# Attention scores from two float32r parts on alternating halves of the array, in place of three bfloat16 parts on 72 rows

## What is computed

```python
h = _layernorm(x, axis=-1) * (1 + ca) + sa
q, k, v = (qkv[0], qkv[1], qkv[2])          # from h @ qkv_w + qkv_b, 16 heads of 8
q = _apply_rotary(q, rope)
k = _apply_rotary(k, rope)
scores = jnp.einsum('bhqd,bhkd->bhqk', q, k) * HD ** (-0.5)
scores = jnp.where(causal_mask, -jnp.inf, scores)
attn = jax.nn.softmax(scores, axis=-1)
out = jnp.einsum('bhqk,bhkd->bhqd', attn, v)
x = x + ga * (out @ out_w + out_b)          # then a second layer norm and the experts
```

## Time and profile before

| | us |
|---|---|
| median of 3 runs | 417.44 |
| lowest, highest | 413.38, 420.29 |
| the profiled execution: its time | 416.36 |
| the profiled execution: its span | 414.6 |
| PE, DVE, ACT, POOL busy in the span | 368.3, 269.7, 219.1, 101.4 |
| mean granted clock of PE, share of full speed | 0.934 |

### The profile page before, as it was taken

How to read it: one execution, slowest core, us unless ns; L and a number is a source line. 1 busy time by engine, 2 the same in 40 slices (tenths; PEclk the granted TensorE clock), 3 DMA queues, 4 the chain that set the end, 5 groups by cost and what they waited for, 6 DMA issues and landing times.

```text
span 414.6 us, 6917 instructions
## 1 busy us (share of the span) xinstructions
PE 368.3 (89%) x2383; PEld 169.0 (41%) x2383; DVE 269.7 (65%) x586; ACT 219.1 (53%) x415; POOL 101.4 (24%) x185
## 2 busy tenths in 40 slices
PE   6948864989879899899999988999999999999876
PEld 3424431444444244333243343444424444434544
DVE  3446781688677747777877777867787777333165
ACT  5240342456215624566767664745776666685333
POOL 3302554245410004232040301200203232213110
PEclk9988996799758959999999999989999999999989
DMA  7276172000110000233304040000000000000000
GB/s 259 97 195 122 64 206 64 3 2 2 63 40 2 0 0 4 90 93 85 91 4 113 3 114 2 3 2 25 3 0 3 4 2 3 3 1 2 25 2 26
DMA packets 12338, 18.87 MB, mean 46 GB/s; under 512 B 3600, under 2 KB 8592, under 8 KB 12176
## 3 DMA queue, kind: packets, MB, share of 16 engines
q1 hardware_dynamic: 12016, 18.04, 15.8%
q10 hardware_dynamic: 288, 0.39, 0.3%
HBM read 12.98 MB, written 5.24 MB: 44 GB/s over the span
## 4 chain that ended last, share of the span: by engine, by line
PE 71%; DVE 7%; issue 5%; ACT 5%; DMA 4%; SPq 4%; POOL 3%; POOLq 0%; ACTq 0%; DVEq 0%
PE ps_o L971 16%; PE ps_b L951 14%; PE ps_a L933 14%; PE ps_a L928 4%; PE ps_a L910 4%; PE ps_s L903 3%; PE ps_s L839 3%; PE ps_s L890 3%; SPq L389 3%; ACT pt L602 2%; DVE tmax L788 2%; DMA qst<-negt 2%; DVE rot L693 2%; PE ps_s L857 1%; PE ps_s L871 1%
## 5 line engine op out<-in xcount | busy, mean ns | idle before, releaser
L788 DVE TENSOR_REDUCE tmax<-ps_a 128x1 f32<-128x512 f32 (+3 forms) x304 | 187.5, 657 | 87.4 <-PE ps_a L933 86.9
L602 ACT ACTIVATE pt<-ps_b 128x512 f32<-128x512 f32 (+1 forms) x304 | 165.5, 573 | 125.2 <-PE ps_b L951 123.3
L951 PE MATMUL ps_b<-qst,kst 75*128 75x512 bf16 (+3 forms) x384 | 116.0, 336 | 12.8 <-DMA qst<-negt 7.7
L933 PE MATMUL ps_a<-kst,qst 72*128 72x128 bf16 (+3 forms) x576 | 118.4, 286 | 1.9 <-DVE tmax L788 1.7
L971 PE MATMUL ps_o<-pt,v_sb 128*32 128x512 f32 (+3 forms) x768 | 84.6, 514 | 0.4 <-POOL pt L498 0.3
L933 PEld LDWEIGHTS ps_a<-kst,qst 72*128 72x128 bf16 x576 | 51.5, 102 | 69.8 <-DVE tmax L788 37.2
L498 POOL TENSOR_SCALAR_AFFINE_SELECT pt<-pt 128x512 f32<-128x512 f32 x64 | 40.2, 636 | 86.6 <-ACT pt L602 86.4
L951 PEld LDWEIGHTS ps_b<-qst,kst 75*128 75x128 bf16 x384 | 35.0, 99 | 44.8 <-ACT pt L602 23.5
L910 PE MATMUL ps_a<-maska,identb 128*128 128x512 bf16 x96 | 29.4, 399 | 3.3 <-POOL maska L435 3.3
L928 PE MATMUL ps_a<-maska,identb 128*128 128x512 bf16 x64 | 26.5, 413 | 4.5 <-DMA kst<-kparts 2.6
L469 POOL CAST negp<-negm 128x16 bf16<-128x16 f32 x16 | 3.1, 196 | 110.7 <-DVE negm L714 110.6
(11 more groups left out here) (108 smaller groups left out, 311.4 us busy)
## 6 DMA issues: line engine op xcount, KB each, us to landing
qst<-qparts SPq DMA_DIRECT2D x48, 96.0 KB
kst<-kparts SPq DMA_DIRECT2D x48, 96.0 KB
qparts<-part SPq DMA_DIRECT2D x4, 384.0 KB, 2.6
kparts<-part SPq DMA_DIRECT2D x4, 384.0 KB, 2.8
xs<-in_x SPq DMA_DIRECT2D x4, 256.0 KB, 6.8
rope_sb<-in_rope SPq DMA_DIRECT2D x1, 1024.0 KB, 6.8
qparts<-part SPq DMA_DIRECT2D x4, 256.0 KB, 2.9
qst<-negt SPq DMA_DIRECT2D x48, 4.0 KB, 1.7
```

The source lines that it names most:

```text
L602: act.activation(pt[:, G % NP, h0:h0 + nh, 0:w], src, ACT.Exp, scale=SCALE).then_inc(s_exp, 1)
L788: dve.tensor_reduce(dst, src, AX.X, ALU.max).then_inc(s_max, 1)
L933: last = pe.matmul(dst[:, j * nk:(j + 1) * nk], qst[0:ROWS, half, h, r * P:r * P + P], kst[0:ROWS, kh, h, k0:k0 + nk], start=(kind != "dia ...
L951: last = pe.matmul(ps_b[:, n % 2, j * w:(j + 1) * w], kst[:, kh, h, kt * P:kt * P + P], qst[:, half, h, c0:HALF], start=True, stop=True)
```

## The change

`PARTS` goes from 3 to 2, and the parts are float32r, a four-byte type of the matmul, to which ACT and POOL round. Two parts of q against two of k give 32 rows a head; a row of zeros follows, and in pass B two rows of the maxima against rows of ones (33 and 35 rows). `qst` and `kst` are float32 now and span 128 partitions: even heads of a group lie from partition 0, odd heads from partition 64 (`a` is the half). A job of pass A and a bank of pass B hold heads of one half only, and the lists alternate: pass A takes half 0, 1, 0, 1, pass B 1, 0, 1, 0 (`ones`), so that in a slot the two stand on different halves. "diag" jobs cover two tiles of two heads instead of one tile of four. Two places that held four heads of 128 columns in one bank take two banks now (tri r=1, and the last key tile of pass B): 12 and 28 jobs a step, 320 of each pass in all.

Stages `q3` and `k3` are gone: two parts need one rounding on ACT and one subtraction. The later prep stages stand earlier in `plan` by as many slots. `load` issues 8 DMAs of 64 KB a group in place of 6 of 96 KB, `max_rows` 4 in place of 3. The rows of ones, which ACT wrote in 3.6 us each for the two halves, come by four DMAs from a small tile on ACT's queue. The transposition of the maxima (`max2`) is float32. Matmuls with v, the masks and all side stages keep their types.

```diff
 NG = H // HG
-PARTS = 3
-ROWS = PARTS * PARTS * HD
-ROWSM = ROWS + PARTS
+PARTS = 2
+SPLIT = PARTS * HD
+ROWS = PARTS * SPLIT
+ROWSA = ROWS + 1
+ROWSB = ROWSA + PARTS
+TILE = 64
+HP = H // 2
 VW = HD + 1
 VPAD = H * VW + 24
 SCALE = float(HD) ** -0.5
 EPS = 1e-5
-ONES = 1 + 0x3F80 / 2 ** 23
...
 def bank_jobs_a(half):
 
-    jobs = []
-    for r in range(TU):
-        jobs.append(("diag", r, 0, HG, P))
-        if r:
-            nh = min(HG, HALF // (r * P)) if r < 3 else 1
-            jobs += [("tri", r, h, nh, r * P) for h in range(0, HG, nh)]
-        if half:
-            jobs += [("sq", r, h, 1, HALF) for h in range(HG)]
+    jobs = [("diag", a, r, 0, 2, P) for r in range(0, TU, 2) for a in range(2)]
+    for r in range(1, TU):
+        nm = 2 if r < 3 else 1
+        jobs += [("tri", a, r, m, nm, r * P) for m in range(0, 2, nm) for a in range(2)]
+    if half:
+        jobs += [("sq", a, r, m, 1, HALF) for r in range(TU) for m in range(2) for a in range(2)]
     return jobs
 
 
 def groups_b(half):
 
     out = []
+    ones = [(2, 1), (0, 1), (3, 1), (1, 1)]
     if half:
-        out += [(kt, 0, 0, [(h, 1) for h in range(HG)]) for kt in range(TU)]
+        out += [(kt, 0, 0, ones) for kt in range(TU)]
     for kt in range(TU):
-        n = HALF - kt * P
-        nh = max(1, HALF // n) if n < 384 else 1
-        out.append((kt, half, kt * P, [(h, nh) for h in range(0, HG, nh)]))
+        out.append((kt, half, kt * P, ones if HALF - kt * P >= 384 else [(2, 2), (0, 2)]))
     return out
...
-PREP = {"norm1": 0, "nz": 2, "hT": 3, "q1": 3, "q2": 3, "q3": 3, "k1": 3, "k2": 3, "k3": 3, "v": 5}
+PREP = {"norm1": 0, "nz": 2, "hT": 3, "q1": 3, "q2": 3, "k1": 3, "k2": 3, "v": 5}
...
+        qst = sb("qst", [P, 2, HP, HALF])
+        kst = sb("kst", [P, 2, HP, HALF])
...
             if name in ("q2", "k2"):
                 i, n = (0, 1)[name == "k2"], prep_no[u]
                 eng.wait_ge(s_full[i], n + 1)
-                eng.wait_ge(s_part[i], 3 * n + 1)
-                eng.tensor_tensor(rot[i][:, 0], full[i][:, :], part[i][:, 0], ALU.subtract).then_inc(s_rem[i], 1)
-            if name in ("q3", "k3"):
-                i, n = (0, 1)[name == "k3"], prep_no[u]
-                eng.wait_ge(s_rem[i], n + 1)
-                eng.wait_ge(s_part[i], 3 * n + 2)
-                eng.tensor_tensor(part[i][:, 2], rot[i][:, 0], part[i][:, 1], ALU.subtract).then_inc(s_part[i], 1)
+                eng.wait_ge(s_part[i], 2 * n + 1)
+                eng.tensor_tensor(part[i][:, 1].bitcast(F32R), full[i][:, :], part[i][:, 0],
+                                  ALU.subtract).then_inc(s_part[i], 1)
...
-                    planes = (5, PARTS)[i]
-                    for p in range(PARTS):
-                        rows = bass.AP(tensor=src, offset=(w * planes * HD + p * step) * row + h0 * HALF,
-                                       ap=[[row, R], [1, HG * HALF]])
-                        sp.dma_start(dst[R * p:R * p + R, half, h0:h0 + HG, :].rearrange("p h t -> p (h t)"),
-                                     rows).then_inc(s_stack[half][g], 16)
+                    planes = (PARTS + 1, PARTS)[i]
+                    for a in range(2):
+                        for p in range(PARTS):
+                            rows = bass.AP(tensor=src, offset=(w * planes * HD + p * step) * row + (HP * a + 2 * g) * HALF,
+                                           ap=[[row, SPLIT], [1, 2 * HALF]])
+                            r = TILE * a + SPLIT * p
+                            sp.dma_start(dst[r:r + SPLIT, half, 2 * g:2 * g + 2, :].rearrange("p h t -> p (h t)"),
+                                         rows).then_inc(s_stack[half][g], 16)
...
-                M = HG * TU
-                for p in range(PARTS):
-                    dst = qst[ROWS + p:ROWS + p + 1, half, HG * g:HG * g + HG, :].rearrange("o h (r x) -> o (h r) x", x=P)
-                    sp.dma_start(dst, negt[M * p:M * p + M, s % 2, :]).then_inc(s_mstack[s % 2], 16)
+                for a in range(2):
+                    for c in range(PARTS):
+                        r, n = TILE * a + ROWSA + c, HP * (PARTS * a + c)
+                        dst = qst[r:r + 1, half, 2 * g:2 * g + 2, :].rearrange("o m (r x) -> o (m r) x", x=P)
+                        sp.dma_start(dst, negt[n:n + HP, s % 2, :]).then_inc(s_mstack[s % 2], 16)
...
             act.wait_ge(s_one, 1)
-            rows_of_ones(0)
+            for a in range(2):
+                r = TILE * a + ROWS
+                act.dma_start(kst[r:r + 1 + PARTS].rearrange("p f h t -> p (f h) t"),
+                              consts[:, :].unsqueeze(1).to_broadcast([1 + PARTS, 2 * HP, HALF])).then_inc(s_ones, 16)
+                act.dma_start(qst[r:r + 1].rearrange("p f h t -> p (f h) t"),
+                              consts[0:1, :].unsqueeze(1).to_broadcast([1, 2 * HP, HALF])).then_inc(s_ones, 16)
...
+                rows = slice(TILE * a, TILE * a + ROWSA)
+                tiles_of = [(q, m) for q in (r, r + 1) for m in range(2)] if kind == "diag" else \
+                    [(r, m0 + j) for j in range(nm)]
+                for j, (q, m) in enumerate(tiles_of):
+                    k0, kh = (q * P, half) if kind == "diag" else (0, half) if kind == "tri" else (0, 0)
+                    last = pe.matmul(dst[:, j * nk:(j + 1) * nk],
+                                     qst[rows, half, 2 * g + m, q * P:q * P + P].bitcast(F32R),
+                                     kst[rows, kh, 2 * g + m, k0:k0 + nk].bitcast(F32R), start=(kind != "diag"),
+                                     stop=True, skip_group_check=True)
...
+                if gi == 0 and (h0, nh) == groups_b(half)[0][3][0]:
+                    pe.wait_ge(s_mstack[s % 2], 64 * (s // 2 + 1))
                 if n >= 2:
                     pe.wait_ge(s_exp, n - 1)
                 for j in range(nh):
-                    h = HG * g + h0 + j
-                    last = pe.matmul(ps_b[:, n % 2, j * w:(j + 1) * w], kst[:, kh, h, kt * P:kt * P + P],
-                                     qst[:, half, h, c0:HALF], start=True, stop=True)
+                    a, m = divmod(h0 + j, 2)
+                    rows = slice(TILE * a, TILE * a + ROWSB)
+                    last = pe.matmul(ps_b[:, n % 2, j * w:(j + 1) * w],
+                                     kst[rows, kh, 2 * g + m, kt * P:kt * P + P].bitcast(F32R),
+                                     qst[rows, half, 2 * g + m, c0:HALF].bitcast(F32R), start=True, stop=True)
...
-                    c = (HG * g + j) * VW
+                    c = (HG * g + 2 * (j % 2) + j // 2) * VW
```

More of the change, by code:

```diff
@@ L26 @@
 F32 = mybir.dt.float32
+F32R = mybir.dt.float32r
 BF16 = mybir.dt.bfloat16
@@ L216, in adaln_block @@
         rank = sb("rank", [P, TU, NE])
-        ones = sb("ones", [P, 1])
+        consts = sb("consts", [1 + PARTS, HALF])
         mhalf = sb("mhalf", [P, TU])
@@ L239, in adaln_block @@
         full = [sb(f"full{i}", [P, HALF]) for i in range(2)]
-        part = [sb(f"part{i}", [P, PARTS, HALF], BF16) for i in range(2)]
-        qst = sb("qst", [ROWSM, 2, H, HALF], BF16)
-        kst = sb("kst", [ROWSM, 2, H, HALF], BF16)
+        part = [sb(f"part{i}", [P, PARTS, HALF]) for i in range(2)]
+        qst = sb("qst", [P, 2, HP, HALF])
+        kst = sb("kst", [P, 2, HP, HALF])
         v_sb = sb("v_sb", [P, B * 2 * TU, VPAD])
@@ L284, in adaln_block @@
         s_part = [sem(f"s_part{i}") for i in range(2)]
-        s_rem = [sem(f"s_rem{i}") for i in range(2)]
         s_store = [sem(f"s_store{i}") for i in range(2)]
@@ L515, in _ @@
             act.activation(sig[:, 0], ct_sb[:, :], ACT.Exp, scale=-1.0).then_inc(s_exp0, 1)
-            def rows_of_ones(half):
-                rows = kst[64:ROWSM, half].rearrange("p h t -> p (h t)").bitcast(F32)
-                act.activation(rows, ones[64:ROWSM].to_broadcast([ROWSM - 64, H * HALF // 2]),
-                               ACT.Copy).then_inc(s_ones, 1)
             act.wait_ge(s_one, 1)
-            rows_of_ones(0)
+            for a in range(2):
[4 more added lines that the diff above has]
+                              consts[0:1, :].unsqueeze(1).to_broadcast([1, 2 * HP, HALF])).then_inc(s_ones, 16)
             def affine(st, dst, which, cols=slice(0, HALF)):
@@ L544, in run @@
                         act.wait_ge(s_store[i], (2, 1)[i] * 16 * n)
[L545 to L551 removed]
+                    act.activation(part[i][:, 0].bitcast(F32R), full[i][:, :], ACT.Copy).then_inc(s_part[i], 1)
                 if name == "max2":
@@ L929, in pass_a @@
                               skip_group_check=True)
-                for j in range(nh):
-                    h = HG * g + h0 + j
-                    k0, kh = (r * P, half) if kind == "diag" else (0, half) if kind == "tri" else (0, 0)
-                    last = pe.matmul(dst[:, j * nk:(j + 1) * nk], qst[0:ROWS, half, h, r * P:r * P + P],
-                                     kst[0:ROWS, kh, h, k0:k0 + nk], start=(kind != "diag"), stop=True,
```

(3 more changed lines are left out.)

92 lines of the change are left out of this document (42 added, 50 removed).

## The result

The changed kernel takes 535.8 us (median of 4 runs, 535.1 to 549.5) where the kernel before takes 416.8 beside it: a ratio of 1.285, interval 1.276 to 1.293. It is 119 us slower; the forecast was 13 us faster and its range ended at 440. Several kernels here have an execution that is two to five per cent slower at a lower clock (549.5 is one), so kernels are compared by the others, and from the profiles of a_filler and a_noturns, which are of such slower executions, only steps at one granted clock are read.

What follows compares the result with a forecast made beforehand. PE was taken to bound the kernel, in a chain of PE, ACT, PE per group. Terms -14 - 5 + 5 + 2 + 3 - 2 - 2 = -13 on 416.4 gave 403, forecast 404 us; range 394 to 440.

Steps and rivals of the forecast that it cites:

- the fourth rival: Clock or DVE takes the gain back, PE idling more; 27 us more at half clock: 417 us, chance 0.17.
- The sign that I had named: A time above 426 us would mean the price or overlap of the new matmuls was not what was taken.
- Price of a column, overlap: Pass A and B matmuls: 512 float32r columns cost 0.22 us as in bfloat16; row halves run side by side.
- The first two rivals: Pass A and B: halves don't overlap, 444 us, chance 0.13; or float32r at half rate, 435 us, chance 0.15.
- 64 x 0.22: 64 four-bank groups: pass B's first bank starts 0.22 us earlier, period 3.10 to 2.88, -14 us in all.
- Weights: 128-column matmuls each bring their own weights, slower in float32: 29 us uncovered, nothing if covered; taken as +2 us.
- The third rival: Diagonal jobs: 128-column matmuls cost 0.22 us as float32 does; 429 us (418 to 435), chance 0.12.
- Switches: 64 mask matmuls on all 128 rows between matmuls on 64: 0.24 us each, 15 us uncovered; taken as +5 us.
- The other 32 I count at nothing: 32 of the 96 groups, diagonal and short, were counted as gaining nothing from pass A and B starting together.
- one issue more: One added DMA issue for the maxima, 0.6 us, at the earlier trace's long wait; -2 us in all there.
- Prologue: Preparation chain before the first pass A: two steps go, two DMA issues added; -2 us (-3 to +0.5).
- Slots: 304 jobs become 320 of each pass, banks of 512 become two of 256: DVE 418, ACT 384 ns; +3 us.

Runs made afterwards that it cites:

- a_filler: The changed kernel with a full-height bfloat16 mask matmul ahead of every triangle and square job of pass A: 546.2 us, clock 0.868.
- a_noturns: The changed kernel with both matmuls of a slot on the same half, so that no two halves overlap: 599.2 us, clock 0.649.
- b_rows33: The kernel before with 33 rows in pass A and 36 in pass B in place of 72 and 75, bfloat16, no halves: 529.1 us, ratio 1.265.
- b_rows33_pad: The kernel before with 32 rows of pairs, filled up with rows of zeros to 125 and 128 rows: 408.5 us, ratio 0.982.
- b_pad: The kernel before, all nine products kept, filled up with rows of zeros from 72 and 75 to 125 and 128 rows: 409.5 us, ratio 0.985.
- a_rows64_2st: The changed kernel, float32r, with 62 and 64 rows (added ones zero) and two DMAs for the maxima in place of four: 472.6 us, ratio 1.127.
- a_rows64: The changed kernel with 62 and 64 rows in place of 33 and 35, the added ones zero: 505.8 us, ratio 1.216.
- a_2st: The changed kernel, with its own 33 and 35 rows, with two DMAs for the maxima in place of four: 541.8 us, clock 0.706.
- a_bf16_rows64: The changed kernel with bfloat16 parts and 62 and 64 rows, the added ones zero, four DMAs for the maxima: 450.5 us, ratio 1.080.

## Why the prediction was wrong, point by point

**The step that failed is the clock.** The sum was made at the clock of before, "Mean clock still 0.93", and the fourth rival, which lets the clock take the gain back, took as its cause that PE "stands idle more often" and as its size "27 us more at half clock". What the runs show is 232 us more at half clock, the longest spell with PE busy nearly throughout, and a cause that neither case had: the rows. PE's matmuls take nearly twice as long there (v 1.86 against 1.00), so these 232 us hold up to 116 us of lost time (an estimate), nearly all of the 119. The earlier trace rows showed PE standing still and then a low clock, and I took that for the only way. The change cuts the rows of 960 matmul instructions from 72 and 75 to 33 and 35, which I priced at nothing. That the rows do this is shown by b_rows33 against b_rows33_pad, 529 and 408 us, on the array as a whole; on halves, where 64 rows are all there are, 62 and 64 rows bring part of it back. The sign that I had named was wrong too: above 426 us it was to be "the price or the overlap of the new matmuls", and at 535.8 us both were what I took for 512 columns.

**A ladder** puts the rest in order (medians; each step but the first has one edit; the kernel before took 416.8 to 421.6 us beside these runs, so a step is good to some 5 us):

| from | to | us |
|---|---|---|
| kernel before, filled up (b_pad) | halves, bfloat16, 62 and 64 rows, two DMAs | 409.5 to 426.8 |
| the same | in float32r (a_rows64_2st) | 426.8 to 472.6 |
| the same | with four DMAs (a_rows64) | 472.6 to 505.8 |
| the same | with 33 and 35 rows (the changed kernel) | 505.8 to 535.8 |

The steps don't add in every order: with 33 and 35 rows the four DMAs cost nothing (a_2st), since PE at half clock comes late anyway. In the other order, with two DMAs, the rows are worth 69 us (472.6 to 541.8), not 30. The first step holds halves, parts, fewer rows and one DMA less at once.

**Price of a column, overlap: right.** Two 512-column matmuls of pass B in float32r record 0.73 together where one records 0.50, so the second starts 0.23 after the first, one column a cycle at 2.4 GHz as for bfloat16; and A and B start at the same time. The first two rivals, no overlap and half rate, are out. The term "64 x 0.22" was right too for what it named: in bfloat16 the group goes from 3.10 to 2.91. In float32r the type takes it back: 3.13.

**Weights: mis-sized, and in the wrong place.** I took +2 of a possible 29 and had no float32r term for the groups. Measured at the full clock, 2.3 us a half 1 step and 1.5 a half 0 step (10.05 against 8.55, and three more like it): 8 x 2.3 + 8 x 1.5 = 30 us, an estimate, since only four half 0 steps and some of the half 1 steps are clean. It comes in two parts. Six groups a half 1 step at 0.22 are 1.3. Four diagonal jobs are the other 1.0, as the timeline of the changed kernel shows at the full clock:

```profile
362.16 0.39 PE L924 MATMUL ps_a<-maska,identb 128*128 128x512 bf16 x1
...
362.49 0.44 PE L949 MATMUL ps_b<-qst,kst 35*128 35x384 f32 x1
...
362.64 0.50 PE L931 MATMUL ps_a<-kst,qst 33*128 33x128 f32 x3
...
363.07 0.39 PE L924 MATMUL ps_a<-maska,identb 128*128 128x512 bf16 x1
```

From mask to mask it is 0.91, where a_bf16_rows64 has 0.64 and the kernel before 0.67: 0.06 more for each 128 columns with weights of their own, near the 0.075 that the upper end was made of. Pass B's one matmul beside it, a record of 0.44, doesn't cover it. The third rival (0.22 each) is out. Of the remaining 16 us of the ladder's 46, 7.8 come before the first step's maxima (56.98 against 49.19): PE waits 12.2 us for the first load of k in place of 6.2. The changed kernel, without the added rows of zero, waits 4.5 there, so this looks like the price of bringing those rows in at four bytes, and not of the matmuls. The rest fits the lower clock, 0.895 against 0.919.

**Switches: there, and paid for by an overlap that I had left out.** A diagonal slot of the kernel before, from mask to mask, then one in bfloat16 on halves (a_bf16_rows64), timelines:

```profile
320.25 0.39 PE L928 MATMUL ps_a<-maska,identb 128*128 128x512 bf16 x1
...
320.48 0.39 PE L933 MATMUL ps_a<-kst,qst 72*128 72x128 bf16 x4
...
320.70 0.38 PE L951 MATMUL ps_b<-qst,kst 75*128 75x512 bf16 x1
...
320.92 0.38 PE L928 MATMUL ps_a<-maska,identb 128*128 128x512 bf16 x1
```

```profile
306.93 0.39 PE L924 MATMUL ps_a<-maska,identb 128*128 128x512 bf16 x1
...
307.25 0.23 PE L931 MATMUL ps_a<-kst,qst 62*128 62x128 bf16 x1
...
307.26 0.33 PE L949 MATMUL ps_b<-qst,kst 64*128 64x384 bf16 x1
...
307.57 0.39 PE L924 MATMUL ps_a<-maska,identb 128*128 128x512 bf16 x1
```

The slots last about the same, 0.67 and 0.64. But from the mask to pass A it is 0.32 where it was 0.23, and from pass A, with pass B beside it, to the next mask 0.32 where four matmuls of 0.055 are 0.22. So each change of height costs some 0.10, 0.20 a mask, near the 0.24 that I had worked out (64 x 0.20 = 13 us, an estimate). What covers it is pass B beside pass A in the diagonal slots, 0.22 each, which the sum counted at nothing ("The other 32 I count at nothing"). Their net is near 0; that +5 isn't far from it is luck.

**The maxima's DMAs: placed at one point, and met at every step.** I counted "one issue more" at the wait of the earlier trace rows alone. In the kernel before PE waits for three DMAs a step 1.3 us in all outside that wait; four, at 0.64 us each instead of 0.59, come late in eight to ten places of the 16 steps with 62 and 64 rows. Two in place of four are worth 33 us (float32r, 62 and 64 rows) or 24 us (bfloat16). The waits themselves are 13 and 16 us of that (15.2 to 2.1, 21.3 to 5.5); the rest goes with a higher clock (0.835 to 0.895, 0.879 to 0.919). Three on halves wasn't tried. In the changed kernel PE's longest wait for them is 3.3 us, where it was 6.4.

**Prologue: the first matmul isn't its end.** The first pass A came at 28.72 against 29.17 (27 forecast). The store of q was issued 2.4 us earlier, but took 5.73 us to land in place of 2.95, as the two chains show, before and after:

```profile
19.79 2.95 DMA qparts<-part
```

```profile
17.42 5.73 DMA qparts<-part
```

The first step's maxima came at 47.83 against 41.49. Windows from the first pass A to them, before and after:

```profile
29.17:41.49 12.32, 11.28 (x54) 5.71 (x55) 7.74 (x13) 0.93 (x2) 2.41 (x2) 0.79 0.69 125
```

```profile
28.72:47.83 19.11, 18.96 (x58) 9.22 (x59) 9.21 (x16) 0.63 (x1) 3.36 (x3) 0.76 0.40 118
```

PE is busy in 18.96 of the 19.11 us, so it isn't the 32 loads in place of 24 that hold this up, but PE's own work. The first three diagonal slots, at half clock, take 2.0 us each, where a slot took 1.3 (float32r weights again); the projections of the next unit, moved ahead by the shorter preparation, take 1.8 us before the maxima are due, and last 3.6 us in place of 2.6 at their first place, in half clock. I had looked for the end of the prologue at the first matmul: -2 became +6 at the first maxima.

**Slots**: DVE 416 and ACT 383 ns for the new 256-column banks, as worked out (418, 384). Right.

One rule of the Trainium skill bears on the failed step. "TensorE: Matmul & The Clock Gate", Part 1, says that the ratio of the clock is set by how busy PE has been recently. The trace doesn't agree if busy is what the profile counts: the window at 242 shows PE busy in 4.00 of 4.00 us at 0.50. The measurement decides.

**What stays open.** Which matmul lifts the clock again, and why b_rows33 found the full clock at 389 us and kept it with the same few rows, isn't known; no run here tells it. How the first step of the ladder, 17 us, divides wasn't tried alone: the first step's maxima come 6.6 us later there (49.19 against 42.57), and the clock is 0.919 against 0.958. Why the store of q took longer to land in the prologue isn't known either.

## What to carry to other kernels

Fewer rows per matmul are no saving on a PE that is already bound by streaming: they save no column, and here the clock was at half for 54% of the span; where K is short, filling up with rows of zero to 128 left a clean step as it was (21.84 us), cost some microseconds of prologue, and is worth a run. Before splitting an operand into halves or a wider type, count the DMA issues and weight loads that come with every step, not with the first one, and look which of them lands just in time now. When PE's clock is low in a window, read PE's busy share beside it: low with PE idle and low with PE busy need different cures.

## What was not expected of the hardware

- The mean granted clock followed the rows that a matmul instruction uses, whatever they hold, though with the same few rows there were long stretches at either level: 0.727 with 33 and 36 rows, 0.934 with 72 and 75, 0.958 with the latter filled up with zeros to 125 and 128, and 0.975 for the former filled up; on two halves in float32r 0.731 with 33 and 35, 0.835 with 62 and 64.
- Two matmuls on opposite row halves start at once and both stream a column a cycle, in bfloat16 and float32r (209.20 and 209.20). A change between full-height and half-height matmuls takes 0.10 us each way.
- In these kernels float32r streams like bfloat16 but costs 0.12 us more from the start of pass B to its exponential (0.57 against 0.45) and 0.11 more before v (0.43 against 0.32), and its weight loads show as 0.18 against 0.09 to 0.10.
